# Two loads move to ScalarE's queue, one warm-up matmul fewer, and another order of the last three scalings in a role adapter with layernorm

## What is computed

```python
h = jnp.einsum('bsh,bhk->bsk', hidden_states, W_down[role]) + b_down[role][:, None, :]
h = jax.nn.gelu(h, approximate=False)
u = jnp.einsum('bsk,bkh->bsh', h, W_up[role]) + b_up[role][:, None, :]
y = hidden_states + u
mean = jnp.mean(y, axis=-1, keepdims=True)
var = jnp.mean(jnp.square(y - mean), axis=-1, keepdims=True)
yn = (y - mean) * jax.lax.rsqrt(var + LN_EPS)
return yn * gamma[role][:, None, :] + beta[role][:, None, :]
```

## Time and profile before

| what | us |
|---|---|
| median of three runs | 362.35 |
| lowest and highest | 362.23, 362.87 |
| the profiled execution, its own time | 362.48 |
| its span | 360.7 |
| PE busy | 353.2 |
| DVE busy | 285.6 |
| ACT busy | 185.0 |

### The profile page before, as it was taken

The page is one execution under the profiler, slowest core; times in us unless marked ns, Lnnn a source line. Parts: engine busy times, 40 slices in busy tenths (PEclk is TensorE's granted clock), DMA queues, the critical chain, the costliest instruction groups (busy, mean ns, idle before and its releaser), DMA issues.

```text
span 360.7 us, 4991 instructions
## 1 busy us (share of the span) xinstructions
PE 353.2 (98%) x1559; PEld 290.2 (80%) x1559; DVE 285.6 (79%) x301; ACT 185.0 (51%) x303; POOL 59.8 (17%) x75
## 2 busy tenths in 40 slices
PE   9999999999999999999999999999999999999992
PEld 4888888888888888888888888888888888888882
DVE  3788999298993989759996699957989489893886
ACT  4785556761368415682256814476234862255133
POOL 0000222003220213102140022300232003320003
PEclk9999999999999999999999999999999999999999
DMA  6999999962999549994699927999099981745023
GB/s 187 393 408 409 410 393 358 355 237 87 333 336 362 219 121 370 330 344 172 172 363 343 353 107 244 341 360 352 40 297 348 377 315 53 240 147 204 1 115 120
DMA packets 27804, 96.61 MB, mean 268 GB/s; under 512 B 3218, under 2 KB 3858, under 8 KB 27794
## 3 DMA queue, kind: packets, MB, share of 16 engines
q1 hardware_dynamic: 23186, 81.14, 62.8%
q10 hardware_dynamic: 4608, 15.34, 11.0%
HBM read 79.70 MB, written 16.78 MB: 267 GB/s over the span
## 4 chain that ended last, share of the span: by engine, by line
PE 92%; DVE 3%; ACT 2%; issue 1%; POOL 1%; POOLq 0%; DVEq 0%; ACTq 0%
PE down_ps L311 48%; PE up_ps L318 42%; DVE rows L683 1%; PE up_ps L432 1%; DVE rows L688 1%; ACT squares L488 1%; DVE rows L742 0%; POOL rstd L603 0%; DVE up_ps L720 0%; POOLq L44 0%; ACT h_full L478 0%; ACT h_hi L480 0%; ACT neg_mean_scaled L485 0%; POOL var_eps L601 0%; DVE down_ps L705 0%
## 5 line engine op out<-in xcount | busy, mean ns | idle before, releaser
L311 PE MATMUL down_ps<-x_hi,wd_hi 128*128 128x512 f32 x256 | 81.2, 390 | 0.1
L311 PE MATMUL down_ps<-x_lo,wd_hi 128*128 128x512 f32 x256 | 80.9, 389 | 0.0
L311 PE MATMUL down_ps<-x_hi,wd_lo 128*128 128x512 f32 x256 | 80.8, 389 | 0.0
L318 PE MATMUL up_ps<-wu_hi,h_hi 128*128 128x512 f32 x248 | 76.4, 389 | 0.0
L318 PE MATMUL up_ps<-wu_lo,h_hi 128*128 128x512 f32 x248 | 76.4, 389 | 0.0
L318 PE MATMUL up_ps<-wu_hi,h_lo 128*128 128x512 f32 x248 | 76.3, 389 | 0.0
L601 POOL TENSOR_TENSOR var_eps<-var,eps 128x1 f32<-128x1 f32 x31 | 22.7, 733 | 292.0 <-ACT squares L488 292.0
L485 ACT ACTIVATE neg_mean_scaled<-row_sum 128x1 f32<-128x1 f32 x31 | 6.3, 203 | 124.7 <-DVE rows L688 124.7
L676 DVE TENSOR_TENSOR h_lo<-h_full,h_hi 128x512 fp32r<-128x512 f32 x32 | 22.2, 693 | 46.6 <-ACT h_hi L480 46.6
L311 PEld LDWEIGHTS down_ps<-x_hi,wd_hi 128*128 128x128 f32 x256 | 47.9, 188 | 11.1 <-issue 0.9
L311 PEld LDWEIGHTS down_ps<-x_hi,wd_lo 128*128 128x128 f32 x256 | 48.0, 188 | 10.0
(11 more groups left out here) (64 smaller groups left out, 274.2 us busy)
## 6 DMA issues: line engine op xcount, KB each, us to landing
wu_stage<-W_up SPq DMA_DIRECT2D x32, 512.0 KB, 7.0
rows<-x SPq DMA_DIRECT2D x32, 512.0 KB, 7.4
x_stage<-xT SPq DMA_DIRECT2D x30, 512.0 KB, 7.1
wd_stage<-W_down SPq DMA_DIRECT2D x30, 512.0 KB, 8.6
out<-rows ACTq DMA_DIRECT2D x28, 512.0 KB, 4.6
b_up_row<-b_up SPq DMA_DIRECT2D x8, 512.0 KB, 5.1
gamma_row<-gamma SPq DMA_DIRECT2D x8, 512.0 KB, 9.5
beta_row<-beta SPq DMA_DIRECT2D x8, 512.0 KB, 10.3
```

The lines of the kernel that those rows point to most:

```text
L311: return pe.matmul(down_ps[:, kc, :], wd_part[:, n, c * K + kc * P:c * K + (kc + 1) * P], x_part[:, n, c * S:(c + 1) * S], start=start, st ...
L318: mm = pe.matmul(up_ps[:, t % 2, half], h_part[:, kc, t * P:(t + 1) * P], wu_part[:, kc, half], start=(kc == 0 and h_part is h_hi and wu_p ...
```

## The change

ACT's queue now waits for the roles and reads the first one right behind its Gelu on the small tile, and issues the third and the fourth load of W_down; SP's queue no longer does. The role read there is also used for the bias of the first batch, so the later read is gone. One warm-up matmul is left out. At the end, DVE scales `POOL_PIECE` second instead of third, with a semaphore of its own (`pool_part_scaled`) for which ACT waits.

```diff
-    WARM_UP = 11
+    WARM_UP = 10
...
+        pool_part_scaled = sem("pool_part_scaled")
...
+        def wd_src(role):
+            return W_down[role].rearrange("(n p c) k -> p n (c k)", n=NLOAD, c=CPL)
...
             load_first_wd(0, slice(0, P), early_wd_landed)
             load_first_wd(0, slice(P, EARLY), second_wd_landed)
-            load_first_wd(0, slice(EARLY, K), first_wd_landed[0])
-            load_first_wd(0, slice(K, CPL * K), wd_landed[0])
             load_first_x(1, 0, first_x_landed[1])
...
             def scale_last_columns():
                 t = NT - 1
-                act.wait_ge(scaled, NT * B + 2)
+                act.wait_ge(pool_part_scaled, 1)
                 act.wait_ge(rstd_ready, NT * B)
...
-            def first_steps():
-                role = load_role(act, 0)
+            def first_steps(role):
...
             act.wait_ge(constants_ready, 2)
             act.activation(unused[:, :], eps[:, :], ACT.Gelu)
+
+            act.wait_ge(roles_landed, 16)
+            first_role = load_role(act, 0)
+            act.dma_start(wd_stage[:, 0, EARLY:K], wd_src(first_role)[:, 0, EARLY:K]).then_inc(first_wd_landed[0], 16)
+            act.dma_start(wd_stage[:, 0, K:CPL * K], wd_src(first_role)[:, 0, K:CPL * K]).then_inc(wd_landed[0], 16)
             round_first(x_hi, x_stage, 0, slice(0, S), first_x_landed[0], first_x_hi)
...
-            act.wait_ge(roles_landed, 16)
             act.wait_ge(b_down_landed, 16)
-            first_steps()
+            first_steps(first_role)
...
-                for i, part in enumerate(LAST_PARTS):
+                for i, ready in ((0, scaled), (2, pool_part_scaled), (1, scaled)):
 
                     dve.wait_ge(part_var_ready, i + 1)
                     dve.scalar_tensor_tensor(out=LAST_BANKS[i], in0=LAST_BANKS[i], scalar=neg_shift[:, :],
-                                             in1=gamma_row[:, part], op0=ALU.add, op1=ALU.mult).then_inc(scaled, 1)
+                                             in1=gamma_row[:, LAST_PARTS[i]], op0=ALU.add, op1=ALU.mult).then_inc(ready, 1)
```

More of the change, by code:

```diff
@@ L188, in _ @@
         def _(sp):
-            def wd_src(role):
-                return W_down[role].rearrange("(n p c) k -> p n (c k)", n=NLOAD, c=CPL)
             def load_x_part(batch, i):
```

## The result

| | before | after |
|---|---|---|
| median of 22 runs each, us | 362.64 | 363.58 |
| lowest and highest, us | 362.23, 363.11 | 362.88, 367.53 |
| the profiled execution, us | 362.48 | 366.57 |
| its span, us | 360.7 | 364.7 |

The ratio is 1.0047, with a 95% interval of 1.0032 to 1.0061: slower by half a percent, outside the range of the prediction. The spread is part of the result. Before, all runs lie within 0.9 us; after, nine of 22 are over 364.4 us, and even the lowest, 362.88, is 0.65 above the lowest of before. The profiled execution is one of the nine.

What follows compares the result with a forecast made beforehand. PE, busy 92% of the span, was taken to bound the kernel, leaving gains only at its start and behind its last matmul. Gains 0.0 + 0.25 + 0.1 = 0.35 us gave 362.0 us, range 361.4 to 363.0.

Steps and rivals of the forecast that it cites:

- The warm-up matmul, 0.0 us: Start: dropping the eleventh warm-up matmul shortens nothing, since the rounding that ended at 4.86 held matmul 1; 0.0 us.
- Rival (c): Start: PE idles after ten warm-ups, clock taken back or not yet given; 1.6 us more, 363.9; chance 0.05.
- ACT's queue is free beside the table load: Start: ACT's queue reads the role at 1.9 us, issues at 2.76 and 3.29; x rounded from 3.63, 0.18 late.
- Rival (a): Start: ACT's queue stands behind the table load, x rounded from 4.7 or 4.9; 362.55 to 362.9 us; chance 0.22.
- The 0.67 us from the rows at 310 us: ACT's time from role read (310.6) to next instruction (311.27), taken as the delay after the early read.
- Matmul 1 later by 0.15, at most 0.25: First down matmul: the third load beside the small pieces delays it 0.15 us, bounds 0 and 0.25.
- The second piece: no term at all: W_down's second 64 KB piece, needed early in the down matmuls: the forecast gave its landing no delay term.
- The fourth load: gain of 0.25: Matmuls 13 to 17: fourth load issued at 3.29, landing near 7.1, nearly removes the stall; 0.25 us gained.
- Rival (b): Start: DMA engines, not issue, set the fourth load's landing; rounded by about 8.1, only the end gains; 362.25; chance 0.15.
- The order of scalings, 0.1: End: POOL's part scaled earlier, so ACT starts at about 356.5 instead of 356.62; gain 0.1 us.
- The sum: Whole kernel: 0.0 + 0.25 + 0.1 = 0.35 us faster, 362.0 us; chance 0.50.

Runs made afterwards that it cites:

- loads alone: Kernel before with only the third and fourth load of W_down moved to ACT's queue (eleven warm-up matmuls, old order of scalings): 362.82 us against 362.63.
- order alone: Kernel before with only the last three scalings in the new order: 362.74 us against 362.63.
- the changed kernel's second profile: Changed kernel run again unchanged, beside its variants: median 363.51 us against 362.63 of the kernel before; the profiled execution took 364.85 us.
- fourth load alone: Kernel before with only the fourth load of W_down on ACT's queue, the third still in SP's row: 364.31 us against 362.74.
- SP held back: Kernel before with both loads on ACT's queue, SP waiting for the second small piece before its further loads: 363.31 us against 362.74.
- foreign transfers: Kernel before, SP issuing all four loads, plus two unused transfers of 128 and 256 KB on ACT's queue: 365.27 us against 362.63.

## Why the prediction was wrong, point by point

The step that failed is the price of the bytes on ACT's queue for W_down's two small pieces: 0.15 us for the first, no term for the second. The first came 0.7 us late, the second 3.0, and in this execution the second one's wait was followed by a fall of the clock.

**The warm-up matmul, 0.0 us.** Right alone (0.1, not told from zero), too good beside the other edit. I named its cover, the rounding of the first piece, and then let the loads lengthen that cover without asking what PE's longer idle time does. Rival (c) had both forms, the clock taken back and the clock not yet given, and a chance of 0.05. The two profiles of the changed kernel show one each: 1.3 us of a loss of 4.1, and most of 1.6 us (all that was lost behind the start of matmul 1) of a loss of 2.5. Of the other runs of the tail it isn't known. That its number, 363.9, is near the median is luck, since it left out the late pieces. The moment of the rise differs between executions, as the Trainium skill's TensorE: Matmul & The Clock Gate, section on the HAM clock gate, says. The traces agree (from under 3.6 us to about 10), and I used that for a chance only.

**ACT's queue is free beside the table load.** Right. The view of the roles' tile after:

```profile
L168 ACTq TENSOR_LOAD <-roles_sb x8: 289/292/481, 1.9 to 314.6; - x8
```

It reads at 1.9 us and issues at 2.85 and 3.37 (forecast 2.76 and 3.29); x is rounded at 3.75 (3.63). Rival (a) falls. The 0.67 us from the rows at 310 us were partly luck: ACT worked on the squares until 311.15 there, so those rows bound the time after a read and do not measure it.

**Matmul 1 later by 0.15, at most 0.25.** The term that failed. The five profiles with both loads moved, SP not held back and ten or eleven warm-up matmuls have it at 5.63 to 5.91, later by 0.6 to 0.9. I put 64 KB of foreign bytes ahead of the piece and divided by the mean rate. Between 4 and 5 us the DMA engines were full (share 1.00) at 274 GB/s, and not at 100 with a share of 0.34 as before. At that rate the 0.7 us of delay are some 190 KB, an estimate from these two numbers: three times what I had counted, of the 384 KB that ACT had issued.

**The second piece: no term at all.** I priced the delay of the first piece and took the second with it. It was the dearest where it was late: 3.2 and 4.9 us to land instead of 1.9, and matmul 3 late by 1.2 (loads alone, at 6.76) and 2.8. With both loads moved and eleven warm-up matmuls it took 2.7 us in an execution of 362.86, near the median, so 4.9 us is a case of the tail.

**The fourth load: gain of 0.25.** No gain is visible. The load was issued 0.8 us earlier, yet in the seven profiles with both loads moved it is rounded at 6.88 to 9.06, and in the five with SP's row as before at 6.82 to 7.46. The 7.46 that I started from was the latest of its kind, so part of the stall that I wanted to win was scatter: with the order alone, matmul 13 starts at 7.92. The earliest with moved loads (eleven warm-up matmuls):

```profile
6.88 0.62 ACT L450 CAST wd_hi<-wd_stage 128x512 fp32r<-128x512 f32 x1
```

ACT did not wait for it there, nor with the loads alone (7.44): it was busy with the pieces ahead of it in its own order, so the late small pieces hold the fourth load's rounding too. Rival (b) had the outcome for this load, and was too mild, since it took the sharing to be harmless to the others. The rule that I weighed there, from the Trainium skill's DMA: Bandwidth & Descriptors, section "Issuing engines are not separate DMA queues", is that transfers of several issuers interleave. The traces agree with it: 2.3 to 3.2 us for the first piece beside ACT's loads, 1.9 to 2.0 without. I read it as a cap on the gain and not as a loss for what was first in the row.

**The order of scalings, 0.1.** Right in the trace at 0.08.

**The sum.** Forecast -0.35, measured +0.94 in the median. From the runs, the moved loads cost 0.2 to 0.3 us with eleven warm-up matmuls (362.82 and 362.96 against 362.63). With ten instead of eleven the median is 0.55 higher on the same chip (363.51 against 362.96), by a tail rather than by a shift: without the runs over 364.2, on all chips, the medians are 363.05 with ten and 362.86 with eleven. On that chip alone the 0.55 is not clear of noise.

## What to carry to other kernels

A first load that PE waits for is served best by a queue in which everything behind it is really behind it. Moving later loads to a second queue wins their issue time (0.5 us each here) and takes away their place: they and the pieces that they meet delayed each other here, so ask of every early transfer what else is in flight beside it. Where a warm-up bridges PE to its first operand, judge its length together with everything that makes this operand later, and by the spread of many runs, not by one profile.

## What the runs showed of the hardware that was not expected

- The first 64 KB piece landed after 1.9 to 2.0 us with nothing of another queue beside it (five profiles), and after 2.3 to 3.2 us with 128 to 384 KB of another queue issued up to 0.9 us behind it (ten profiles). For the second piece it was 1.9 to 2.7 and 2.5 to 4.9 us.
- With ten or eleven warm-up matmuls, the spacing of matmuls fell from 0.43 to about 0.22 us at moments from under 3.6 us (order alone) to about 10 (the changed kernel's second profile, after a pause).
- The granted clock in the record read 1.00 at a spacing of 0.43 us before the first rise, and 0.50 at that spacing after a fall: only the spacing tells the first case.
- After an idle time of 1.94 us PE ran at 1.2 GHz until about 11.8 us; after one of 0.43 (loads alone, ahead of matmul 3), 1.17 (fourth load alone) and 1.34 us (SP held back, both ahead of matmul 1) it stayed at 2.4 GHz. The fall need not come in the pause: behind an idle time of 1.49 us (foreign transfers) matmul 3 started at 7.87 still fast, and the granted clock fell at about 8.4.
